# Reordering the work between the last scans and the first softmax groups of a four-layer sequence kernel

## The reference: what is computed

```python
x = x + gate * mamba(layernorm(x) * (1 + scale) + shift)          # layer 0, 16 states, one direction
x = x + gate * (W_f(silu(mx) * (ssm1(z1) + flip(ssm2(flip(z2))))) + skip)   # layer 1, both directions
# layer 2: linear attention with 16 heads of 16 channels
q = softmax(xn @ Wq + bq, over the 16 channels of a head)
k = softmax(where(mask, -inf, xn @ Wk + bk), over the 1024 tokens)
v = where(mask, 0, xn @ Wv + bv)
y = q @ (k.T @ v)                                                 # one 16 x 16 matrix for each head
x = x + silu(layernorm(y) * (1 + scale) + shift) @ W_out + b_out  # the FiLM
# layer 3: full softmax attention, 16 heads, mask added to the scores
y = softmax(q @ k.T + (1 - mask) * -1e6) @ v
x = x + silu(layernorm(y) * (1 + scale) + shift) @ W_out + b_out
```

## Time and profile before

| | |
|---|---|
| median of 3 runs | 2120.67 us (2118.75 to 2123.79) |
| the profiled execution | 2122.75 us, span 2121.0 us |
| busy PE / DVE / ACT / POOL | 1739.7 / 1822.9 / 1211.9 / 1147.5 us |
| critical chain by engine | PE 40%, DVE 34%, issue 9%, POOL 8%, ACT 7% |
| last scan ends | about 1460.8 us from the span's start |
| first softmax group begins | about 1680 us |
| mean granted TensorE clock | 0.889 |

### The profile page before, as it was taken

One profiled execution on the slowest core, in us unless ns is written; L12 is line 12 of the kernel. 1 busy time (PEld: TensorE's weight loads), 2 busy tenths in 40 slices (PEclk: granted clock), 3 DMA queues, 4 the chain that ended last, 5 costly groups with the idle time before them and its releaser, 6 DMA issues.

```text
span 2121.0 us, 23810 instructions
## 1 busy us (share of the span) xinstructions
PE 1739.7 (82%) x8210; PEld 651.4 (31%) x8210; DVE 1822.9 (86%) x2159; ACT 1211.9 (57%) x2171; POOL 1147.5 (54%) x585
## 2 busy tenths in 40 slices
PE   5788879678797888678788888796897899999985
PEld 2222213132231323232322222232663333333323
DVE  4699999899999999999998999999547888888803
ACT  3766465645656666555565666543452266666672
POOL 2688877877888887789898787764000000000000
PEclk9898979869697899899997999887998799999998
DMA  6152522222223232322222232331061522220001
GB/s 198 56 160 79 95 71 75 66 61 71 75 70 98 79 95 80 87 70 72 91 81 88 74 100 73 108 90 46 1 121 39 83 33 32 32 32 2 2 2 40
DMA packets 95941, 149.83 MB, mean 71 GB/s; under 512 B 24291, under 2 KB 31651, under 8 KB 95412
## 3 DMA queue, kind: packets, MB, share of 16 engines
q1 hardware_dynamic: 95820, 148.31, 27.1%
HBM read 137.05 MB, written 10.62 MB: 70 GB/s over the span
## 4 chain that ended last, share of the span: by engine, by line
PE 40%; DVE 34%; issue 9%; POOL 8%; ACT 7%; DMA 2%; SPq 0%; DVEq 0%; ACTq 0%; POOLq 0%
DVE hbuf L2331 19%; DVE hbuf L2312 7%; PE psum L1721 6%; PE psum L731 6%; POOL hbuf L1421 6%; PE psum L697 5%; PE psum L717 4%; PE psum L612 3%; PE psum L1510 3%; DVE gain L1012 2%; PE psum L601 2%; PE psum L1673 1%; PE psum L1518 1%; PE psum L1537 1%; DMA cbuf<-scr_c 1%
## 5 line engine op out<-in xcount | busy, mean ns | idle before, releaser
L1421 POOL TENSOR_TENSOR hbuf<-hbuf,cbuf 128x1024 f32<-128x1024 f32 x384 | 901.8, 2358 | 272.9 <-DVE hbuf L2331 141.2
L2119 ACT ACTIVATE psum<-slots,cols 128x512 f32<-128x512 f32 x708 | 485.5, 689 | 392.0 <-DVE hbuf L2331 387.9
L1721 PE MATMUL psum<-hbuf,ident 64*64 64x512 f32 x3072 | 491.6, 715 | 172.8 <-POOL hbuf L1421 172.2
L2312 DVE TENSOR_TENSOR hbuf<-slots,psum 128x1024 f32<-128x1024 f32 x354 | 422.1, 1193 | 49.8 <-POOL slots L1338 30.3
L2331 DVE TENSOR_TENSOR_SCAN hbuf<-psum,hlast,hbuf 128x512 f32<-128x512 f32 x354 | 432.5, 1263 | 8.7 <-ACT psum L2119 8.7
L2331 DVE TENSOR_TENSOR_SCAN hbuf<-psum,hbuf 128x512 f32<-128x512 f32 x354 | 411.1, 1200 | 8.8 <-ACT psum L2119 8.8
L1012 DVE TENSOR_REDUCE gain<-psum 128x1 f32<-128x512 f32 x512 | 315.4, 680 | 59.2 <-PE psum L697 58.7
L563 POOL COPY wl<-hbuf 128x512 f32<-128x512 f32 x8 | 4.8, 613 | 429.1 <-PE psum L731 400.4
L697 PE MATMUL psum<-slots 99*128 99x512 bf16 x512 | 197.1, 400 | 23.9 <-DVE gain L1012 11.5
L717 PE MATMUL psum<-slots 102*128 102x512 bf16 x512 | 194.5, 388 | 6.5 <-ACT xn_flat L895 1.7
L1721 PEld LDWEIGHTS psum<-hbuf,ident 64*64 64x64 f32 x3072 | 91.0, 147 | 318.3 <-POOL hbuf L1421 255.4
(11 more groups left out here) (278 smaller groups left out, 2234.3 us busy)
## 6 DMA issues: line engine op xcount, KB each, us to landing
cbuf<-scr_c SPq DMA_DIRECT2D x384, 256.0 KB, 3.2
slots<-scr_qk SPq DMA_DIRECT2D x96, 128.0 KB
wl<-scr_diag SPq DMA_DIRECT2D x18, 256.0 KB, 4.7
scr_qk<-slots SPq DMA_DIRECT2D x8, 512.0 KB, 2.8
wl<-in_w SPq DMA_DIRECT2D x8, 496.0 KB, 4.9
wl<-in_ada_w SPq DMA_DIRECT2D x1, 3584.0 KB
xt<-in_x SPq DMA_DIRECT2D x2, 1024.0 KB, 12.5
wl<-in_w SPq DMA_DIRECT2D x2, 1024.0 KB, 7.0
```

What stands on the lines that cost most here:

```text
L1421: pool.tensor_tensor(hs, hs, cbuf[:, at % CRING:at % CRING + 1, :].to_broadcast([P, 2, TC]), ALU.mult).then_inc(weighed, 1)
L1721: last = pe.matmul(psum[side, bank, :], ident[rows_of, rows_of], hbuf[rows_of, at % RING, q, :], start=False, stop=n == NS - 1, skip_group ...
L2119: act.activation(decay_bank(at, q), dts[k % 2][:, e, :], ACT.Exp, scale=coefficient(WORK[k], e, n)).then_inc(decay, 1)
L2312: dve.tensor_tensor(hbuf[:, at % RING, :, :], ws[k % 2][:, 2 * p:2 * p + 2, :], psum[:, 2 + at % 2:3 + at % 2, :].to_broadcast([P, 2, TC]) ...
```

## The change

1. `STAGES`: the key projection of batch 1 is cut in two; its pieces 0 and 1 come before the four 2out pieces of batch 0, pieces 2 and 3 behind them. PE issues them in that order.
2. DVE: the last gate (`close_scans`) moves ahead of `mask_keys(0)`. `divide_queries` loses its head sums, which become `sum_queries` and go ahead of `divide_keys(0)`, and stay just ahead of the rest for batch 1.
3. ACT: the `deviation` of batch 1's tokens moves ahead of `outer_out(0)`. DVE: `keep_own_heads(0)` moves ahead of the normalisation of these tokens.
4. `measure` can wait for each pair of tiles: the statistics of y start pair by pair behind ACT's copies, and those of x start pair by pair behind the output additions, which move into `measure` (`add_pair`, `added`).
5. First maxima: 6 tiles are issued between the transposes of batch 1's FiLM and its output product, 2 after each of its first three pairs, 4 after the last; then 4 after each of the twelve projections of layer 3. The DVE order follows it, with the splits after 32 and 48 tiles.

```diff
--- before.py
+++ after.py
@@ -191,8 +191,10 @@
 
 
 STAGES = []
-for _name, _b in (("2k", 0), ("2m", 0), ("2qT", 0), ("2xT", 1), ("2y", 0), ("2q", 1), ("2hT", 0), ("2out", 0), ("2kT", 1),
-                  ("3xT", 0), ("3q", 0), ("3k", 0), ("2v", 1), ("2k", 1), ("2m", 1), ("2qT", 1), ("2y", 1), ("3v", 0),
+for _name, _b, _pieces in (("2k", 0, 4), ("2m", 0, 1), ("2qT", 0, 4), ("2xT", 1, 4), ("2y", 0, 4), ("2q", 1, 4), ("2hT", 0, 4)):
+    STAGES += [(_name, _b, i) for i in range(_pieces)]
+STAGES += [("2kT", 1, i) for i in range(2)] + [("2out", 0, i) for i in range(4)] + [("2kT", 1, i) for i in (2, 3)]
+for _name, _b in (("3xT", 0), ("3q", 0), ("3k", 0), ("2v", 1), ("2k", 1), ("2m", 1), ("2qT", 1), ("2y", 1), ("3v", 0),
                   ("2hT", 1), ("2out", 1), ("3xT", 1), ("3q", 1), ("3k", 1), ("3v", 1),
                   ("3hT", 0), ("3out", 0), ("3hT", 1), ("3out", 1)):
     STAGES += [(_name, _b, i) for i in range(1 if _name == "2m" else 4)]
@@ -672,8 +674,12 @@
             attend(0)
             after_act("2xT", 1, 3)
             to_tokens("2q", 1, L2[1].xT, w2[:, 0], BQ2)
-            film("2", 1, 0, L2[0].y, L2[0].hT, w2[:, 3], OB2)
-            project("2kT", 1, w2[:, 1], L2[1].xT)
+            pe.wait_ge(h_ready, 1)
+            to_wide("2hT", 0, L2[0].y)
+            project("2kT", 1, w2[:, 1], L2[1].xT, (0, 1))
+            after_act("2hT", 0, 3)
+            to_tokens("2out", 0, L2[0].hT, w2[:, 3], OB2)
+            project("2kT", 1, w2[:, 1], L2[1].xT, (2, 3))
             pe.wait_ge(ld_w23, 32)
             turn_x3(0)
             project("3q", 0, w3[:, 0], x3T[0])
@@ -684,7 +690,8 @@
             turn_queries(1)
             attend(1)
             to_tokens("3v", 0, x3T[0], w3[:, 2], BV3)
-            film("2", 2, 1, L2[1].y, L2[1].hT, w2[:, 3], OB2)
+            pe.wait_ge(h_ready, 2)
+            to_wide("2hT", 1, L2[1].y)
 
             def max_tile(job, i, n):
 
@@ -744,17 +751,21 @@
                     max_tile(0, n // (2 * QH), n % (2 * QH))
 
             start_max(0)
-            find_first(range(4))
+            find_first(range(6))
+            after_act("2hT", 1, 3)
+            for pair in range(TT // 2):
+                to_tokens("2out", 1, L2[1].hT, w2[:, 3], OB2, (pair,))
+                find_first(range(6 + 2 * pair, 8 + 2 * pair if pair < 3 else 16))
             turn_x3(1)
-            at = 4
+            at = 16
             for name, w in (("3q", w3[:, 0]), ("3k", w3[:, 1]), ("3v", w3[:, 2])):
                 for i in range(4):
                     if name == "3v":
                         to_tokens(name, 1, x3T[1], w, BV3, (i,))
                     else:
                         project(name, 1, w, x3T[1], (i,))
-                    find_first(range(at, at + 5))
-                    at += 5
+                    find_first(range(at, at + 4))
+                    at += 4
             turn_max(0)
             start_max(1)
             for i in range(LEAD - TT):
@@ -851,8 +862,8 @@
             exp_queries(0)
             exp_keys(0)
             tokens_out("2k", 0, L2[0].k)
+            deviation()
             outer_out(0)
-            deviation()
             wide_out("2qT", 0, L2[0].qT)
             wide_out("2xT", 1, L2[1].xT, columns=norm_columns(2))
             tokens_out("2y", 0, L2[0].y)
@@ -901,9 +912,11 @@
         def vector_attention(dve, link, close_scans, add_last_out):
             norms = [0]
 
-            def measure(src):
+            def measure(src, have_pair=None):
                 norms[0] += 1
                 for i in range(TT):
+                    if have_pair is not None and i % 2 == 0:
+                        have_pair(i // 2)
                     last = dve.bn_stats(stats[:, i, :], src[:, i, :])
                 link(last)
                 for i in range(TT):
@@ -934,10 +947,13 @@
                     ins = dve.tensor_scalar(m.kT[:, k, :], m.kT[:, k, :], m.k_inv[:, k:k + 1], None, ALU.mult)
                 ins.then_inc(kn_ready, 1)
 
-            def divide_queries(b):
+            def sum_queries(b):
                 m = L2[b]
                 dve.wait_ge(q_exp, b + 1)
                 link(dve.tensor_reduce(m.head_inv, by_head(m.q), AX.X, ALU.add))
+
+            def divide_queries(b):
+                m = L2[b]
                 link(dve.reciprocal(m.head_inv, m.head_inv))
                 dve.tensor_tensor(by_head(m.q), by_head(m.q), over_head(m.head_inv), ALU.mult).then_inc(qn_ready, 1)
 
@@ -946,12 +962,17 @@
                 dve.tensor_tensor(L2[b].outer, L2[b].outer, heads[:, :].rearrange("p (o e) -> p o e", o=1).to_broadcast([P, KD, P]),
                                   ALU.mult).then_inc(outer_ready, 1)
 
+            def add_pair(name, b, pair):
+                xs = tokens_of_batch(b)[:, 2 * pair:2 * pair + 2, :]
+                dve.wait_ge(t_done, T[name, b, pair] + 1)
+                dve.tensor_tensor(xs, stage_bank((name, b, pair)).rearrange("p (q d) -> p q d", q=2), xs, ALU.add).then_inc(t_dve, 1)
+
+            def added(name, b, pair):
+                dve.wait_ge(t_dve, t_taken((name, b, pair)))
+
             def add_out(name, b, signal):
                 for pair in range(TT // 2):
-                    xs = tokens_of_batch(b)[:, 2 * pair:2 * pair + 2, :]
-                    dve.wait_ge(t_done, T[name, b, pair] + 1)
-                    last = dve.tensor_tensor(xs, stage_bank((name, b, pair)).rearrange("p (q d) -> p q d", q=2), xs, ALU.add)
-                    last.then_inc(t_dve, 1)
+                    add_pair(name, b, pair)
                 dve.wait_ge(t_dve, t_taken((name, b, TT // 2 - 1)))
                 if signal is not None:
                     dve.sem_inc(signal, 1)
@@ -972,36 +993,42 @@
             dve.wait_ge(taken_act, taken(G["2kT", 0, 3]))
             link(dve.tensor_scalar(m0.never, m0.mask, 1.0, NEVER, ALU.is_equal, ALU.mult))
             shift_queries(0)
+            close_scans()
             mask_keys(0)
-            close_scans()
+            sum_queries(0)
             divide_keys(0)
             divide_queries(0)
             add_last_out()
             measure(tokens_of_batch(1))
+            keep_own_heads(0)
             normalize(tokens_of_batch(1), m1.xn, xn_ready)
-            keep_own_heads(0)
             dve.wait_ge(ld_mask2, 32)
             dve.tensor_scalar(m1.never, m1.mask, 1.0, NEVER, ALU.is_equal, ALU.mult).then_inc(never_ready, 1)
-            dve.wait_ge(t_act, t_taken(("2y", 0, 3)))
-            measure(m0.y)
+
+            def have_y(b):
+                return lambda pair: dve.wait_ge(t_act, t_taken(("2y", b, pair)))
+
+            def add_first_out(pair):
+                add_pair("2out", 0, pair)
+                added("2out", 0, pair)
+
+            measure(m0.y, have_y(0))
             normalize(m0.y, m0.y, h_ready)
             dve.wait_ge(t_act, t_taken(("2q", 1, 3)))
             shift_queries(1)
-            add_out("2out", 0, None)
-            measure(tokens_of_batch(0))
+            measure(tokens_of_batch(0), add_first_out)
             normalize(tokens_of_batch(0), x3[0], xn_ready)
             dve.wait_ge(never_ready, 1)
             dve.wait_ge(t_act, t_taken(("2kT", 1, 3)))
             mask_keys(1)
+            sum_queries(1)
             divide_queries(1)
             split(0, 0)
             divide_keys(1)
             split(1, 0)
             keep_own_heads(1)
-            dve.wait_ge(t_act, t_taken(("2y", 1, 3)))
-            measure(m1.y)
+            measure(m1.y, have_y(1))
             normalize(m1.y, m1.y, h_ready)
-            add_out("2out", 1, None)
 
             def max_half(job, i, n):
 
@@ -1052,13 +1079,20 @@
                 for n in tiles:
                     max_half(0, n // (2 * QH), n % (2 * QH))
 
-            measure(tokens_of_batch(1))
+            def add_second_out(pair):
+                add_pair("2out", 1, pair)
+                if pair < 3:
+                    find_first(range(6 + 2 * pair, 8 + 2 * pair))
+                added("2out", 1, pair)
+
+            find_first(range(6))
+            measure(tokens_of_batch(1), add_second_out)
             normalize(tokens_of_batch(1), x3[1], xn_ready)
-            find_first(range(24))
+            find_first(range(12, 32))
             split(0, 1)
-            find_first(range(24, 44))
+            find_first(range(32, 48))
             split(1, 1)
-            find_first(range(44, 2 * UNITS))
+            find_first(range(48, 2 * UNITS))
             close_max(0)
             split_max(0)
             for i in range(LEAD - TT):
```

## The result

The changed kernel takes 2108.22 us in the median of 5 runs (2102.43 to 2112.58), against 2120.67 (5 runs, 2118.75 to 2123.79) before. The ratio is 0.9931 [0.9908, 0.9954], so it is faster, by 0.5 to 0.9%. Forecast were 2106.2 us and a range of 2099 to 2114.5.

What follows compares the result with a forecast made beforehand. PE and DVE were taken to bound the stretch by turns, waiting for each other, with PE's clock falls. Gains 0.5 + 0 + 3.55 + 2.3 + 8.2 = 14.5 us took 2120.67 to 2106.2 us, range 2099 to 2114.5.

Steps and rivals of the forecast that it cites:

- A: End of the scans: gate ahead of key mask saves 2.2 us of DVE idling, less 1.7 for one clock fall; net 0.5.
- B: Deviation ahead of the outer product's copy, head filter ahead of the normalisation: zero, with 0.3 us either way.
- C: First FiLM: two key projections fill PE's 3.05 us gap, keep the full clock and hide six statistics; 3.55 us gained.
- D: Second FiLM: six maxima tiles fill the 3.30 us gap, six statistics hide under the product; 2.3 us, bounds 0.6 and 4.0.
- E: Layer 3 projections with tiles: twelve fewer reductions (7.4 us) and 0.8 more, steps of 2.6 us; 8.2 gained.
- the fifth's wait: In the projection steps: five tiles on four PE banks make the fifth wait for a reduction; four tiles remove that wait.
- The groups: The 64 groups that begin after the changed stretch: own order untouched, so no gain of their own.
- R1: PE's clock follows the gaps, falling also at 1528.2 and not kept by D's tiles: gain 11.1, 2109.6 us; chance 0.15.
- R2: First stack's loads land too late for the earlier tiles in the second FiLM, product 5 us late: 2111.2 us; chance 0.08.
- R3: The clock is kept in A, after the splits and in D: 2100 to 2101 us; chance 0.14.
- R4: E's steps stay at 3.1 us because something other than the fifth tile sets them: gain 8.5, 2112.2 us; chance 0.07.
- R5: Groups begin at another phase of the clock's falls, seven job ends cost 24 us: slower, 2130 us; chance 0.04.

Runs made afterwards that it cites:

- gate_alone: Kernel before with only the last gate ahead of the key mask and head sums ahead of the key division; stretch 206.12 us, 1.54 longer than before.
- late_wait: Changed kernel with PE's wait for DVE's last two additions moved from ahead of the key transposes to ahead of the first maxima; stretch 189.46 us.
- four_moves: all_three with ACT's deviation again behind the outer product's copy; 2093.92 us, ratio to before 0.9868, stretch 181.64 us.
- gate_back: Changed kernel with the last gate again behind the key mask and the head sums behind the key division; stretch 192.95 us.
- gate_back_late_wait: late_wait with the last gate again behind the key mask; stretch 189.49 us against 189.46.
- after_again: The changed kernel profiled once more, unaltered; stretch 193.24 us, 191.72 in its first profile.
- five_steps: Changed kernel with five maxima tiles to a projection instead of four, splits behind 36 and 56; x3 to joined maxima 52.91 us, 53.29 in after_again.
- gap_empty: Changed kernel with the six tiles taken out of the second FiLM's gap and six later steps taking five tiles; stretch 197.25 us.
- tiles_back: Changed kernel with the first maxima as before, no tiles in the second FiLM, five after each projection; 2116.61 us, ratio to before 0.9966.
- all_three: Changed kernel with late_wait's move and value pairs issued in the gaps ahead of x3 and in the second FiLM; 2097.39 us, ratio to before 0.9873.

## Why the prediction held, step by step

**A, gate: the mechanism right, the price of the gap too small.** The key transposes came 2.26 us sooner by DVE (19.64 against 21.9), as forecast (2.2), the output product 4.5. The fall was forecast, and a gap of 3.1 us, which is what after's profile has (3.10). But the 3.1 rests on before's 9.99 us for the output product; in the five other profiles with this code it takes 8.8 to 9.0, and the gap is 4.0 to 4.2. The charge of 1.7 was one fall on the transposes (3.33, so 1.4); that the outer product also stays low was only the bound, and is the usual case (5.5 to 5.9 us, 6.05 in gate_alone, against 3.84). Result -0.4 in five of six profiles with this code, +1.1 in one, where 0.5 was forecast.

**B, deviation and filter: 0 forecast, 0 found in after** (the step to `2hT 0` is 18.03 us from `2qT 0`, 18.11 before), but for a reason that held only there. late_wait showed the wait of 4.97 us, and four_moves that it costs 1.85 as soon as the path ahead is faster. I priced DVE's queue behind the copy and not ACT's queue ahead of it.

**C, first FiLM: 3.55 forecast, 2.6 found.** Up to x3 the gain is 3.31 (24.50 to 21.19). The term that failed is the price of the new gap: none charged, since a gap of 1.86 us had kept the clock. That of 2.15 didn't (3.38 against 1.94), of whose price 0.73 reached `2qT 1` in after and 2.14 in gate_back and late_wait. The length alone doesn't decide it: gate_back_late_wait has the same gap and lost nothing.

**D, second FiLM: 2.3 forecast, 0.57 found**, the lower bound (0.6), for the reason that stood beside it. The six tiles didn't keep the clock, first pair 3.59. Here the Trainium skill, TensorE: Matmul & The Clock Gate, section "A second HAM failure mode: psum-queue depth-cycling", was the better guide than my sum. The traces of after, after_again and five_steps agree with it (first pair 3.59, 3.53 and 3.42); gate_back, late_wait and gate_back_late_wait, with the same six tiles, don't (first pair 1.99, and 2.26 us gained), so it isn't a rule without exception here. An empty gap ended low as well (gap_empty, tiles_back).

**E, projections with tiles: 8.2 forecast, 8.57 found.** The mechanism was right, twelve fewer reductions in a stretch bound by them, 7.4 us: tiles_back gave back 8.8, gap_empty 4.0 with half of them. Steps of 2.6 us came as worked out, the waits at the splits at 4.02 and 2.97 (about 4 and 3). The 0.8 credited to "the fifth's wait" wasn't that: five tiles to a step are as fast (52.91). Its working was loose, too: 60 x 0.62 is 37.2 and not 37.0, and PE's wait at the second split was 5.28 and not 5.8. (The 205 us that the prediction starts from end at the joined maxima, 1665, and not at 1680.)

**The groups: 0 forecast, about 2.3 found.** In before, gate_alone and tiles_back they take 440.5 to 440.7 us behind the first exponential, in all with tiles in the film 437.8 to 438.4 (five_steps 439.5). The low clock over the first groups' tiles is there as before (PEclk 0.50, as in the earlier trace rows). Windows of after (busy of PE, PEld, DVE, ACT, POOL; PEclk; DMA share; GB/s):

```profile
1655.00:1665.00 10.00, 10.00 (x20) 2.38 (x20) 10.00 (x18) 1.87 (x4) 0.00 (x0) 0.50 1.04 153
```

But the first weighing product starts 7.5 to 7.6 us behind the first exponential in the former kernels and 6.4 to 6.7 in the latter. That is about 1 us of the 2.3. Why, and where the rest lies, wasn't tried and stays open.

**The sum.** In the usual profile -0.4 + 2.6 + 0.6 + 8.5 = 11.3, and 2.3 of the groups, is 13.6; forecast were 14.5. The medians differ by 12.5, and the ratio with its interval gives 14.6 (9.8 to 19.5). That the total came so near is partly luck: the falls in A, C and D cost 3.5 more than charged, and the groups, which I had put at nothing, with 0.3 of E gave 2.6 back. **R1** (the clock follows the gaps, gain 11.1) describes the stretch better than my forecast did. **R2** didn't happen, with about 4 us of margin. **R3** happened nowhere in after; four_moves comes near it up to the second FiLM. **R4** is refuted by the steps of 2.58 us. **R5** wasn't seen: no kernel's groups were more than 0.2 us longer than before's.

## What to carry to other kernels

Cut both traces at events with the same meaning before explaining a total: here 5.2 of 20.3 us lay in code that nobody touched. Price a gap that a change opens on PE by the work behind it, all of it up to where the clock is back, and take the time of the work in front of it from a row at the same clock. Fill it with matmuls that wait for nobody: the two gaps filled so, ahead of the first output product and of x3's transposes, ended at the full clock each time, while the one filled with tiles paced by DVE ended low in some kernels and full in others. When work is moved out of a bound stretch, the gain is the bound engine's time per piece (0.62 us for each reduction), however the rest is dealt out.

## What the runs showed of the hardware

- The granted clock isn't a function of a gap's length alone. The same gap of 2.15 us was followed by 16 transposes in 3.38 us in after and in 1.94 in gate_back_late_wait; six tiles in the second FiLM's gap by a pair in 3.59 (after) and by one in 1.99 (gate_back). A fall at x3's transposes cost from 0.7 to 2.1 us of the path. What decides it stays open: untouched stages changed when an earlier one moved by 0.4 us (after_again, gate_back), and didn't when one moved by 1.5 (after, after_again).
- A stack whose twelve loads of 128 KB were issued from 1554.10 was whole by 1570.16, 16.1 us from the first's issue, with twelve more loads queued behind (all_three).
- The scan part of 1460 us varies by 12.6 us between profiles of kernels that share its code, 1455.57 to 1468.22 us. This is most of what spreads the totals, and a single total can't show a change of 4 us.
